# Decoder block with routed experts: routed rows scattered to DRAM and loaded turned, in place of row transposes on TensorE

## The reference

```python
x = x + attention(layernorm(x))          # 16 heads of 128, soft-capped scores, causal, gated
x = x + experts_by_token_id(layernorm(x))  # 4 experts, one by token id: y = (silu(h C.T) * (h C.T)) C.T
x = x + moe(layernorm(x))

def moe(h):                              # h: 2048 rows of 512
    probs = softmax(h @ gate_w.T)        # 8 experts
    w, selected = top_k(probs, 2); w = w / (w.sum(-1) + 1e-20)
    out = (silu(h @ shared_gate.T) * (h @ shared_up.T)) @ shared_down.T     # inner 704
    for each row and each of its two experts e:
        out += w_e * (silu(h @ gate_e.T) * (h @ up_e.T)) @ down_e.T         # inner 352
    return out
```

## Time and profile before

| | |
|---|---|
| time, three runs | 1577.18, 1578.02, 1578.02 us; median 1578.02 |
| the profiled execution | 1577.97 us, its span 1576.2 us |
| busy: TensorE, its weight load | 1555.3 us (99%), 1332.2 us (85%) |
| busy: VectorE, ScalarE, GpSimd | 1040.1 us (66%), 583.2 us (37%), 454.0 us (29%) |
| granted clock of TensorE | 1.00 |
| expert stage | from about 1289 us to 1562 us of the span |
| DMA traffic | 353.28 MB |

### The profile page before, as it was taken

One profiled execution on the slowest core, in us unless ns is written; L12 is line 12 of the kernel. 1 busy time (PEld: TensorE's weight loads), 2 busy tenths in 40 slices (PEclk: granted clock), 3 DMA queues, 4 the chain that ended last, 5 costly groups with the idle time before them and its releaser, 6 DMA issues.

```text
span 1576.2 us, 23814 instructions
## 1 busy us (share of the span) xinstructions
PE 1555.3 (99%) x7776; PEld 1332.2 (85%) x7777; DVE 1040.1 (66%) x2230; ACT 583.2 (37%) x997; POOL 454.0 (29%) x390
## 2 busy tenths in 40 slices
PE   7999999999999999999999999999999999999998
PEld 5888888888888888888888888888888889999997
DVE  4798877788887788886787778755663662222222
ACT  4444443434444334444344344333212213333232
POOL 4445332134222233222233221113200013332431
PEclk9999999999999999999999999999999999999999
DMA  8786764677876686985686877366440256677643
GB/s 294 280 314 222 231 222 137 238 291 261 305 286 221 243 313 233 309 311 196 246 308 250 307 280 307 118 218 198 131 151 9 110 209 199 192 238 241 193 80 74
DMA packets 106804, 353.28 MB, mean 224 GB/s; under 512 B 11280, under 2 KB 31760, under 8 KB 101200
## 3 DMA queue, kind: packets, MB, share of 16 engines
q1 hardware_dynamic: 93488, 314.20, 55.4%
q0 software_dynamic: 13216, 37.79, 10.2%
HBM read 227.97 MB, written 123.98 MB: 223 GB/s over the span
## 4 chain that ended last, share of the span: by engine, by line
PE 92%; DVE 3%; DMA 2%; issue 1%; POOL 1%; ACT 1%; SPq 0%; DVEq 0%; ACTq 0%; POOLq 0%
PE bank L370 30%; PE bank L372 29%; PE bank L371 29%; PE bank L1984 1%; PE bank L2104 1%; DMA out<-x_early,ids_e 1%; DMA wqk<-wqk_parts 0%; DMA rows<-x_rows,ids_e 0%; DMA resid<-x 0%; POOL store L691 0%; DVE resid L1498 0%; DMA resid<-out 0%; DVE place_hot L1661 0%; DVE tile_vals L1671 0%; PE bank L2061 0%
## 5 line engine op out<-in xcount | busy, mean ns | idle before, releaser
L733 POOL TENSOR_TENSOR probs<-probs,causal 128x256 f32<-128x256 f32 x126 | 90.2, 737 | 408.9 <-ACT probs L913 408.9
L372 PE MATMUL bank<-store,wqk 128*128 128x512 f32 x512 | 202.1, 395 | 0.0
L370 PE MATMUL bank<-store,wqk 128*128 128x512 f32 x512 | 201.8, 394 | 0.2 <-DMA wqk<-wqk_parts 0.2
L371 PE MATMUL bank<-store,wqk 128*128 128x512 f32 x512 | 201.8, 394 | 0.0
L1304 DVE SCALAR_TENSOR_TENSOR resid<-bank,factor,resid 128x512 f32<-128x512 f32 x256 | 189.2, 741 | 1.2 <-PE bank L372 1.1
L691 POOL TENSOR_TENSOR pre_split<-pre_raw,pre_split 128x1528 fp32r<-128x1528 f32 x34 | 120.3, 3539 | 142.8 <-ACT pre_split L875 142.8
L911 ACT ACTIVATE probs<-bank 128x512 f32<-128x512 f32 x189 | 85.9, 529 | 130.8 <-PE bank L372 130.8
L372 PEld LDWEIGHTS bank<-store,wqk 128*128 128x128 f32 x512 | 96.0, 188 | 22.8
L371 PEld LDWEIGHTS bank<-store,wqk 128*128 128x128 f32 x512 | 96.1, 188 | 20.8
L370 PEld LDWEIGHTS bank<-store,wqk 128*128 128x128 f32 x512 | 96.0, 188 | 20.2 <-DMA wqk<-wqk_parts 0.4
L1335 DVE TRANSPOSE_TENSOR_REDUCE bank<-probs 128x16 f32<-128x512 f32 (+3 forms) x256 | 108.4, 492 | 0.0
(11 more groups left out here) (352 smaller groups left out, 3927.0 us busy)
## 6 DMA issues: line engine op xcount, KB each, us to landing
pre_parts<-pre_split SPq DMA_DIRECT2D x34, 1528.0 KB, 6.6
wqk<-wqk_parts SPq DMA_DIRECT2D x96, 512.0 KB, 4.9
pre_raw<-pre SPq DMA_DIRECT2D x34, 764.0 KB, 7.8
store<-wv_parts SPq DMA_DIRECT2D x12, 2048.0 KB, 9.1
wo<-wo_parts SPq DMA_DIRECT2D x48, 512.0 KB, 8.3
expert_w<-pre_parts SPq DMA_DIRECT2D x8, 2816.0 KB, 11.4
wqk_parts<-wqk SPq DMA_DIRECT2D x16, 1024.0 KB, 5.1
expert_w<-pre_parts SPq DMA_DIRECT2D x8, 1536.0 KB, 8.8
```

What stands on the lines that cost most here:

```text
L370: nc.tensor.matmul(out_ap, a_hi, b_hi, start=first, stop=False)
L371: nc.tensor.matmul(out_ap, a_hi, b_lo, start=False, stop=False)
L372: return nc.tensor.matmul(out_ap, a_lo, b_hi, start=False, stop=last)
L733: nc.gpsimd.tensor_tensor(diagonal, diagonal, causal[:, :, :], ALU.mult).then_inc(S["masked"], 1)
```

## The change

Tiles 0 to 5 are still gathered and transposed by TensorE. For tiles 6 to 38 every row is scattered to its two places in a new DRAM tensor `es` (GpSimd, 32 indirect DMAs, as soon as the slots are written), from copies of the 16 row tiles that SyncE loads back from `x3_rows` in five pieces; ScalarE issues four turned loads per tile from `es`, four tiles ahead, and VectorE turns the tile into PSUM. `es` is filled with zeros in the first batch (five DMAs of SyncE). The first four gathers stand after the scatters of ten row tiles, the other two after all. There are eight result buffers, and the weight loads wait for products in place of transposes.

```diff
+        staging = sb("staging", [P, 4, D])
+        def staged(t0, t1):
+            if 6 <= t0 < 10:
+                return staging[:, t0 - 6:t1 - 6, :]
+            at = t0 % 10
+            at += LATE_FROM - 3 if at >= 3 else 0
+            return resid[:, at:at + t1 - t0, :]
...
+        es = nc.dram_tensor("es", (ETILES * P, D), F32, kind="Internal").ap()
...
-        E_ROWS, E_AHEAD = 4, 6
+        E_ROWS, E_GATHERED, E_LOADS, FIRST_LOADS = 4, 6, 4, 3
+        STAGED = ((0, 3), (3, 6), (6, 10), (10, 13), (13, 16))
+        GATHERS_FROM = 10
...
-        def load_turned(tile, source, done):
+        def load_turned(tile, source, done, engine=nc.sync):
             for r in range(QUADS):
-                nc.sync.dma_start(tile[r * BLOCK:(r + 1) * BLOCK, :].rearrange("x (a q) -> x a q", a=QUADS),
+                engine.dma_start(tile[r * BLOCK:(r + 1) * BLOCK, :].rearrange("x (a q) -> x a q", a=QUADS),
...
-            fills = [(xs, "zero_filled_x", at) for at in range(0, XTILES, ZTILES)]
+            fills = [(xs, "zero_filled_x", at) for at in range(0, XTILES, ZTILES)] + [(es, "zero_filled_e", at) for at in range(0, ETILES, 2 * ZTILES)]
...
-                for part, used, lo, n in (("up", "e_xT_ready", 0, UP), ("down", "e_aT_ready", UP, DOWN)):
+                for part, used, lo, n in (("up", "e_up", 0, UP), ("down", "e_y", UP, DOWN)):
...
-                        sp.wait_ge(S[used], tiles_before + 1)
+                        sp.wait_ge(S[used], tiles_before)
...
+            def stage(n):
+                t0, t1 = STAGED[n]
+                sp.dma_start(staged(t0, t1), x3_rows[t0 * P:t1 * P].rearrange("(t p) d -> p t d", p=P)).then_inc(S[f"x_tile{n % 3}"], 16)
+
             for n in range(LATE_AT):
+                if n == FULL_STEPS:
+                    for j in range(2):
+                        sp.wait_ge(S[f"x3_stored{j}"], 16 * (TILES // 2))
+                    sp.wait_ge(S["stored"], 16 * (FULL_STEPS + 1))
+                    stage(0)
+                    stage(1)
+                    sp.wait_ge(S["s_up"], 2 * TILES)
+                    stage(2)
+                if n == FULL_STEPS + 5:
+                    sp.wait_ge(scat[0], SCAT_X + 16 * TOPK * 3)
+                    stage(3)
+                if n == FULL_STEPS + 6:
+                    sp.wait_ge(scat[1], SCAT_X + 16 * TOPK * 3)
+                    stage(4)
...
+            def scatter_e(t):
+                for n, (t0, _) in enumerate(STAGED):
+                    if t == t0:
+                        pool.wait_ge(S[f"x_tile{n % 3}"], X_TILE + 16 + 16 * (n // 3))
+                for c in range(TOPK):
+                    nc.gpsimd.indirect_dma_start(es, bass.IndirectOffsetOnAxis(slot_e[:, c, t:t + 1], 0), staged(t, t + 1)[:, 0, :], None).then_inc(scat[min(t // 3, 2)], 16)
...
-                nc.gpsimd.indirect_dma_start(out, bass.IndirectOffsetOnAxis(ids_e[:, g:g + 1], 0), x3_early[:, g % E_ROWS, :], None, compute_op=ALU.add).then_inc(S["e_added"], 16)
+                nc.gpsimd.indirect_dma_start(out, bass.IndirectOffsetOnAxis(ids_e[:, g:g + 1], 0), x3_early[:, g % PT, :], None, compute_op=ALU.add).then_inc(S["e_added"], 16)
...
-            pool.wait_ge(S["ids_ready"], 1)
-            for g in range(E_AHEAD):
+            pool.wait_ge(S["zero_filled_e"], 16 * -(-ETILES // (2 * ZTILES)))
+            pool.wait_ge(S["slots_ready"], TOPK)
+            for t in range(TILES):
+                if t == GATHERS_FROM:
+                    pool.wait_ge(S["ids_ready"], 1)
+                    for g in range(E_ROWS):
+                        gather(g)
+                scatter_e(t)
+            for g in range(E_ROWS, E_GATHERED):
                 gather(g)
             pool.wait_ge(S["stored"], 16 * (LATE_AT + 1))
             for g in range(ETILES):
-                if g + E_AHEAD < ETILES:
-                    gather(g + E_AHEAD)
                 add_rows(g)
...
-                if g >= E_ROWS:
-                    act.wait_ge(S["e_added"], 16 * (g - E_ROWS + 1))
-                nc.scalar.activation(x3_early[:, g % E_ROWS, :], bank[YB][:, :], ACT.Copy).then_inc(S["e_y_out"], 1)
+                if g >= PT:
+                    act.wait_ge(S["e_added"], 16 * (g - PT + 1))
+                nc.scalar.activation(x3_early[:, g % PT, :], bank[YB][:, :], ACT.Copy).then_inc(S["e_y_out"], 1)
...
+            def load_turned_e(g):
+                if g == E_GATHERED:
+                    act.wait_ge(S["stored"], 16 * (LATE_AT + 1))
+                    for n, tiles in enumerate((3, 3, TILES - 6)):
+                        act.wait_ge(scat[n], SCAT_X + 16 * TOPK * tiles)
+                if g >= E_GATHERED + E_ROWS:
+                    act.wait_ge(S["e_xT_ready"], g - E_ROWS + 1)
+                if g >= E_GATHERED + 2:
+                    act.wait_ge(S[f"x3_turned{g % 2}"], TURNED_X3 + 16 * QUADS * ((g - E_GATHERED) // 2))
+                load_turned(resid[:, g % E_ROWS, :], es[g * P:g * P + P], S[f"x3_turned{g % 2}"], nc.scalar)
...
                 aT_high("e", g)
+                if g == FIRST_LOADS:
+                    for n in range(E_GATHERED, g + E_LOADS):
+                        load_turned_e(n)
+                if FIRST_LOADS <= g < ETILES - E_LOADS:
+                    load_turned_e(g + E_LOADS)
...
+            def turn_e(g):
+                dve.wait_ge(S["e_xT_lo"], g)
+                dve.wait_ge(S[f"x3_turned{g % 2}"], TURNED_X3 + 16 * QUADS * ((g - E_GATHERED) // 2 + 1))
+                turn(resid[:, g % E_ROWS, :]).then_inc(S["e_xT_ready"], 1)
...
+                if ph == "e" and E_GATHERED <= g + 2 < ETILES:
+                    turn_e(g + 2)
...
-                    transpose_rows_e(i, j + 1)
+                    if rows_next:
+                        transpose_rows_e(i, j + 1)
...
-            e_step(0, 1, second=False)
-            by_fours(pe, e_step, 2, ETILES - 2)
+            e_step(0, 1, second=False, rows_next=True)
+            for g in range(2, E_GATHERED - 1):
+                e_step(g // 4, g % 4, rows_next=True)
+            by_fours(pe, e_step, E_GATHERED - 1, ETILES - 2)
             last = ETILES - 1
-            transpose_rows_e(last // 4, last % 4)
```

More of the change, by code:

```diff
@@ L161, in build @@
         tile_vals = sb("tile_vals", [P, TOPK * TILES, 3 * ETABLE], F32R)
+        staging = sb("staging", [P, 4, D])
+        assert sb.at <= second_region + 4 * 2 * KC * SH_WIDTH
+        def staged(t0, t1):
[4 more added lines that the diff above has]
+            return resid[:, at:at + t1 - t0, :]
         NE = EXPERTS * TILES
@@ L272, in build @@
         """ + " ".join(f"{ph}_{n}" for ph in "xse" for n in ("xT_ready", "xT_hi", "xT_lo", "up", "silu", "act", "aT_ready", "aT_hi", "aT_lo", "y", "y_out"))
-        names += " " + " ".join(f"{n}{j}" for n in ("x_row", "e_row", "x_y_stored") for j in range(2))
+        names += " " + " ".join(f"{n}{j}" for n in ("x_row", "x_y_stored") for j in range(2))
         S = {n: sem(n) for n in names.split()}
@@ L344, in build @@
         SH_PIECES = 2 * (2 * KC + 4)
-        E_ROWS, E_AHEAD = 4, 6
+        E_ROWS, E_GATHERED, E_LOADS, FIRST_LOADS = 4, 6, 4, 3
+        STAGED = ((0, 3), (3, 6), (6, 10), (10, 13), (13, 16))
+        GATHERS_FROM = 10
+        SCAT_X, GATH_X, X_TILE = 16 * BATCH, 16 * (TILES // PT), 16
+        TURNED_X3 = 16 * 4 * (TILES - TURNED_FROM) // 2
         LAST_PARTS = ((0, SEQ), (SEQ, SEQ), (2 * SEQ, 2 * P))
@@ L559, in _ @@
                     rows_of, done, at = fills[u - 2]
-                    fill(rows_of, done, at, min(ZTILES, rows_of.shape[0] // P - at))
+                    fill(rows_of, done, at, min(ZTILES if done == "zero_filled_x" else 2 * ZTILES, rows_of.shape[0] // P - at))
                 if u == 2 + len(fills):
@@ L573, in _ @@
                     load_ct(1)
-            sp.wait_ge(S["zero_filled_x"], 16 * len(fills))
+            sp.wait_ge(S["zero_filled_x"], 16 * -(-XTILES // ZTILES))
+            sp.wait_ge(S["zero_filled_e"], 16 * -(-ETILES // (2 * ZTILES)))
             def load_row(ph, source, g, j):
@@ L819, in gather @@
                     pool.wait_ge(S["s_xT_ready"], TILES - 1 + g)
-                else:
-                    pool.wait_ge(S[f"e_row{g % 2}"], 16 * (g // 2))
                 if g >= E_ROWS:
                     pool.wait_ge(S["e_xT_ready"], g - E_ROWS + 1)
-                nc.gpsimd.indirect_dma_start(rows[:, g % E_ROWS, :], None, x3_rows, bass.IndirectOffsetOnAxis(ids_e[:, g:g + 1], 0)).then_inc(S[f"e_row{g % 2}"], 16)
+                nc.gpsimd.indirect_dma_start(rows[:, g % E_ROWS, :], None, x3_rows, bass.IndirectOffsetOnAxis(ids_e[:, g:g + 1], 0)).then_inc(gath[g], 16)
             def add_rows(g):
@@ L1183, in route_slots @@
                 link(nc.vector.tensor_reduce(w.slot_f[:, :], w.above[:, 0:NE].rearrange("p (e t) -> p t e", e=EXPERTS), mybir.AxisListType.X, ALU.add))
-                link(nc.vector.tensor_copy(slot_e[:, c, :], w.slot_f[:, :]))
```

(6 more changed lines are left out.)

2 lines of the change are left out of this document (1 added, 1 removed).

## The result

The changed kernel takes 1609.7 us (median of 4 runs, 1608.56 to 1612.06) against 1577.6 for the kernel before: ratio 1.0202, 95% interval [1.019, 1.0214]. It is slower by 32 us, where 1581.1 was forecast and 1589 was the upper end. Its profiled execution took 1610.77 us, with a span of 1609.0, which is 32.8 over the span before.

A forecast was written before the change was run, and what follows sets the result against it. TensorE was taken to bound the expert stage, the serial scatter-adds the kernel's end. 1577.97 - 15.5 (transposes) + 11.3 (adds) + 3.3 (512-byte loads) + 4.0 (late first gather) = 1581.1 us, range 1566 to 1589.

The forecast's parts named there:

- -15.5: Expert stage: row transposes of tiles 6 to 38 leave TensorE, 33 x 0.47 us saved, 15.5 us less.
- Scatters ahead of the first gather: Start: twenty scatters delay the first gather, which falls behind expert 1's weight load; TensorE resumes later, +4.0 us (1.5 to 4.0).
- VectorE stretches the scatters: Start: twenty scatters take 1.20 us each, not 0.97; first gather 4.6 us later, 1585.6 us; chance 0.05.
- my 8.6: Start: time in us from the first gather's issue, behind expert 1's weight load, to the transposes awaiting it; 6.15 before.
- as in my rival: Start: TensorE's clock falls during the 4.9 us wait for first rows, costing 3 us: 1584; chance 0.12.
- Adds: Expert stage's end: serial scatter-adds into `out` fall behind TensorE's results, +11.3 us (0 to 15.5).
- 512-byte term: Expert stage: ScalarE's loads from `es` hold each of 33 adds by 0.1 us, +3.3 (0 to 10.9).
- adds keep up: Expert stage: adds quicken once gathers leave GpSimd's queue, so no backlog: 1566.5 us; chance 0.28.

The follow-up runs named there:

- both costs out: The changed kernel without its 32 scatters into `es` and without ScalarE's 512-byte loads of `es`: 1568.0 us, ratio 0.9935.

## Why the prediction was wrong

The span grew by 32.8 us: add 3 is 27.1 later, adds 3 to 38 take 6.0 longer, the tail is 0.3 shorter. The forecast had +4.0 and -0.9 (-15.5 + 11.3 + 3.3) for the first two.

**The step that failed is "Scatters ahead of the first gather": 27.1 us, not 4.0 with 1.5 to 4.0 as bounds.** Its parts:

- The gather's issue, 8.2 us late in place of 1.5. 1.7 of it was there when the scatters began (1261.03; in other runs of the same stretch 1259.1 to 1261.5). 5.0 are six scatters stretched to 1.2 to 2.6 us, and the rest is the 1.5 of the forecast. The stretch was my rival "VectorE stretches the scatters", to which I gave 0.05, on the one row where a gather ran beside a two-input addition and was not held. That gather had started 0.55 us ahead of the addition, and the scatters show that only one which starts while such an instruction runs is held, until 0.83 us after its end. Instructions with two SBUF inputs fill about 11 of VectorE's 24 us from 1259 to 1283, not nearly all of them. I read the wrong overlap, and the longest scatter shown (1.20) was no bound for a neighbour of 2.29 us. The Trainium skill (SBUF — State Buffer, "SBUF: two separate sides") states a lock: of a VectorE instruction with two SBUF inputs and a GpSimd operation that reads SBUF, the one that starts first has their shared port for its whole length, and the other is blocked. The six of the twenty scatters that started second were held, as it says; but the scatters that started first, 0.26 to 0.75 us ahead, did not hold VectorE (2.29 us in both kernels), and there the measurement decides.
- The landing: 13.6 us from the gather's issue to the transposes, 7.4 more than the 6.15 of before, where I took 8.6. With the weight load held back it was 4.9 at most. Without the scatters a gather issued at 1285.51, 0.7 us behind the same load, landed after 8.2 (by the trace's record of its semaphore), close to my 8.6. So I had half of the cause, from a gather that had no queue of scatters ahead of it: it takes both.
- The late signals, 8.9 us between the transposes and the first product. No part of the prediction has them, and no row of before shows one, since GpSimd's queue is never deep there. The runs with none, two, six and up to 32 in flight show that the depth of the queue sets them, and the stretches above that busy DMA engines do not.
- The clock, 2.5 us, what is left of the 27.1: from the first expert product to add 3 are 36.5 us in place of 34.0. It fell twice, and neither time as in my rival. First before the wait for the first rows, after the wait of 1.97 that a late signal made: the granted clock is 1.00 up to 1290.9 and 0.50 from 1291.1 to 1308, and the matmul at 1290.82 takes 0.61 us in place of 0.39. Then, after 1.00 from 1308.1 to 1311.4, in the wait of 7.76 for the late signal behind the transposes: 0.50 from 1311.6 to 1321.6, so that the first product takes 0.66 us in place of 0.42. This second fall is what the 2.5 us are. The price was near (3 us), by another path than I had described; it came on top of a much longer stall.

**Adds (11.3 late at the end forecast, 14.6 with the 512-byte term).** The last add is 21.1 us behind its result. The mechanism was right: the adds hand back more than TensorE gains. Two sizes were off, in opposite directions. The 512-byte term was 3.3 with 10.9 as upper bound and measured 17.3 (242.5 less 225.2). I had spread it over all adds, where it falls on the dozen that meet weight loads. Without these loads the adds took 225.2 us in place of my 232.3, so the rival "adds keep up" had its point: the adds do get quicker. That the gathers' leaving GpSimd's queue does it is not shown: the weight loads are issued at other moments as well, and no run separates the two.

**What was right.** TensorE's period is 6.24 us (6.27 forecast) with turns that fit, results 3 to 38 come in 221.7 us (221.0 forecast), and the last add is released by the one before. With both costs out the kernel takes 1568.0: 10.9 us of the 15.5 are left there.

What stays open is by what path a deep queue of GpSimd's DMAs holds TensorE's signals. ScalarE, VectorE and GpSimd each saw them late (GpSimd by 8.8 us at 1314.90), while signals between VectorE and ScalarE arrived at once in the same microseconds.

## What to carry to other kernels

Work moved off a saturated TensorE has to pass through what ends the kernel: look first whether the serial chain behind it (here the scatter-adds) has room, and what the new transfers meet there. A burst of indirect DMAs isn't priced by its issue time: what is queued behind it, what runs on VectorE beside it and how many are in flight each cost more than the issues. A bound is only as good as the row's resemblance: ask of each row whether it shows the overlap, the depth and the neighbours that the change will have.

## What the runs showed of the hardware

- With indirect DMAs of GpSimd in flight, TensorE's semaphore signals came late by at most 0.1 us (two scatters in flight), by up to 3.2 (six), and, the late ones among them, by 3 to 40 (up to 32); a burst of 16 gathers made one 12.8 us late.
- A scatter that starts while VectorE runs an instruction with two SBUF inputs ends 0.82 to 0.84 us after that instruction (6 of 6); one that starts 0.26 to 0.75 us ahead of it takes its 0.96 (5 of 5).
- An accumulating scatter that waits for the one before takes 5.2 to 6 us alone, 8 to 12 beside a weight load, and 10 to 12 with the next at 6.6 to 8.8 when 512-byte loads run too. Weight loads in packets of a quarter of the size don't change the sum (241.7 against 242.5 us).
